# Last clipping on ScalarE, a warm-up matmul on a smaller cleared tile, and transfers of the tables in another order

## The reference, cut to what matters

```python
x = _L0_conv_ref(x, ...)   # relu(xWq), relu(xWk), xWv; softmax attention over 256 pixels; + x
x = _L1_conv_ref(x, ...)   # group norm, q, k, v, softmax attention over 256 pixels, Wo; x + h
x = _L2_conv_ref(x, ...)   # attention over 7 hexagonal neighbours, layer norm, feed-forward, layer norm
x = _L3_conv_ref(x, ...)   # 1x1 conv, 3x3 grouped conv, 1x1 conv, each with its affine; see below

# the end of _L3_conv_ref
out = lax.conv_general_dilated(h, w3, (1, 1), 'SAME', dimension_numbers=DN) + b3
return jax.nn.relu(out + x)
```

## Time and profile before

| what | value |
|---|---|
| median of 3 runs | 110.3 us (110.25 to 111.28) |
| the profiled execution, device time | 110.36 us |
| its span, first to last instruction | 108.3 us |
| TensorE matmul busy | 98.4 us |
| VectorE busy | 70.6 us |
| ScalarE busy | 54.2 us |
| GpSimd busy | 31.8 us |
| DMA traffic | 2.88 MB |

### The profile page before, as it was taken

How to read it: one execution, slowest core, us unless ns; L and a number is a source line. 1 busy time by engine, 2 the same in 40 slices (tenths; PEclk the granted TensorE clock), 3 DMA queues, 4 the chain that set the end, 5 groups by cost and what they waited for, 6 DMA issues and landing times.

```text
span 108.3 us, 2233 instructions
## 1 busy us (share of the span) xinstructions
PE 98.4 (91%) x834; PEld 51.9 (48%) x834; DVE 70.6 (65%) x166; ACT 54.2 (50%) x143; POOL 31.8 (29%) x46
## 2 busy tenths in 40 slices
PE   4978899899978999999989999999999998999960
PEld 1435768475646565453822563555322222467420
DVE  2029989989799958999999785498222522200292
ACT  2317969957989799991700400242367454200220
POOL 8960000919547910000004634962000201100000
PEclk9999999999999999999999999999999999999999
DMA  2991000000000000000000000000000000000005
GB/s 82 286 395 60 0 0 0 6 3 3 0 0 0 6 0 0 0 6 0 0 0 0 0 0 6 0 0 0 0 0 0 3 0 9 0 0 6 0 0 194
DMA packets 1594, 2.88 MB, mean 27 GB/s; under 512 B 176, under 2 KB 1200, under 8 KB 1584
## 3 DMA queue, kind: packets, MB, share of 16 engines
q1 hardware_dynamic: 1152, 2.09, 5.4%
q10 hardware_dynamic: 432, 0.67, 2.0%
HBM read 2.23 MB, written 0.52 MB: 25 GB/s over the span
## 4 chain that ended last, share of the span: by engine, by line
PE 54%; DVE 25%; ACT 7%; POOL 5%; issue 5%; POOLq 0%; ACTq 0%; DVEq 0%
PE quad L1097 6%; PE quad L1192 5%; PE bank L1117 4%; PE quad L933 4%; PE quad L1156 4%; DVE probn L672 4%; DVE nmax L663 3%; PE bank L1171 3%; PE bank L944 3%; ACT prob L438 3%; PE duo L1143 3%; PE bank L964 3%; PE duo L1192 3%; DVE ffh L262 2%; DVE ffh L741 2%
## 5 line engine op out<-in xcount | busy, mean ns | idle before, releaser
L438 ACT ACTIVATE prob<-quad,nmax 128x256 f32<-128x256 f32 x32 | 15.0, 483 | 2.5 <-DVE nmax L663 2.3
L944 PE MATMUL bank<-pv,probn 128*128 128x128 f32 x64 | 10.3, 283 | 1.7 <-DVE probn L672 1.1
L663 DVE TENSOR_REDUCE nmax<-quad 128x2 f32<-128x512 f32 x16 | 10.6, 682 | 1.5 <-PE quad L933 1.5
L672 DVE TENSOR_SCALAR probn<-prob,rrec 128x256 f32<-128x256 f32 x32 | 11.1, 390 | 0.6
L445 ACT ACTIVATE probT<-bank 128x512 f32<-128x512 f32 x16 | 9.6, 603 | 3.4 <-PE bank L944 3.2
L944 PEld LDWEIGHTS bank<-pv,probn 128*128 128x128 f32 x64 | 6.9, 141 | 6.1 <-DVE probn L672 3.7
L1192 PE MATMUL quad<-pads,ctaps 32*32 32x512 f32 x144 | 9.2, 595 | 0.0
L1192 PE MATMUL bank<-pads,ctaps 32*32 32x512 f32 x72 | 9.2, 596 | 0.0
L516 ACT ACTIVATE sq<-bank,prep2t 128x512 f32<-128x512 f32 x4 | 2.7, 687 | 12.3 <-PE bank L1117 9.3
L933 PE MATMUL quad<-k,q 32*128 32x256 f32 (+1 forms) x64 | 8.1, 400 | 0.9 <-ACT q L431 0.7
L1192 PE MATMUL duo<-pads,ctaps 32*32 32x512 f32 x72 | 8.8, 593 | 0.0
(11 more groups left out here) (184 smaller groups left out, 206.3 us busy)
## 6 DMA issues: line engine op xcount, KB each, us to landing
p<-in_p SPq DMA_DIRECT2D x1, 1012.5 KB, 7.0
xT<-in_xT SPq DMA_DIRECT2D x4, 128.0 KB, 4.0
p<-in_p ACTq DMA_DIRECT2D x1, 448.0 KB, 5.1
out_dram<-xT SPq DMA_DIRECT2D x1, 256.0 KB, 2.1
out_dram<-xT SPq DMA_DIRECT2D x2, 128.0 KB, 1.7
pv<-in_pv ACTq DMA_DIRECT2D x1, 128.0 KB, 3.2
p<-in_p ACTq DMA_DIRECT2D x1, 74.5 KB, 3.0
```

The costliest lines, as they stand in the source:

```text
L438: s.activation(prob[:, n % 3, b, :], S_BANK[n % 4][:, b * TOK:(b + 1) * TOK], ACT.Exp, bias=nmax[:, n, b:b + 1], accum_out=rsum[:, n, b:b ...
L663: v.tensor_reduce(nmax[:, n, :], S_BANK[n % 4].rearrange("p (b m) -> p b m", b=BLK), AX.X, ALU.max, negate=True).then_inc(max_ready, 1)
L672: v.tensor_scalar(probn[:, n % 2, b, :], prob[:, n % 3, b, :], rrec[:, n, b:b + 1], None, ALU.mult).then_inc(norm_done, 1)
L944: ins = nc.tensor.transpose(T_BANK[:, mb * TOK + b * 128:mb * TOK + b * 128 + 128], probn[:, n % 2, b, mb * 128:mb * 128 + 128], ident)
```

## The change

Three edits stand together.

- The clipping of the last results moves from VectorE to ScalarE. VectorE keeps the addition and raises a new semaphore `x3_sb`; ScalarE waits for it, clips with a Relu, and raises `fin_sb`.
- The tile `zeros` is cleared in two instructions, first 128 columns and then the other 520. The warm-up matmul waits for the first alone and reads those 128 columns four times as its moving operand of 512 columns.
- The pack pv is issued by SyncE between the second and third piece of x, no longer by ScalarE. On ScalarE p1 is issued behind the load of the activation table, no longer ahead of it.

```diff
@@ block.sync @@
             for j in range(PAIRS):
                 sp.dma_start(xT[:, j, :], xd[:, j, :]).then_inc(x_in[j], 16)
+                if j == 1:
+                    sp.dma_start(packed["pv"][:, :], t["pv"]).then_inc(tables_in["pv"], 16)
             sp.dma_start(packed["p2"][:, :], t["p2"]).then_inc(tables_in["p2"], 16)
@@ block.scalar @@
-            for p in ("p0", "pv", "p1"):
-                act.dma_start(packed[p][:, :], t[p]).then_inc(tables_in[p], 16)
+            act.dma_start(packed["p0"][:, :], t["p0"]).then_inc(tables_in["p0"], 16)
             s.preload_act_table_set("natural_log_exp_and_others")
+            act.dma_start(packed["p1"][:, :], t["p1"]).then_inc(tables_in["p1"], 16)
...
+            def finish(n):
+                columns = RESULTS[n][1]
+                act.wait_ge(x3_sb, n + 1)
+                s.activation(fin[:, columns], x3[:, columns], ACT.Relu).then_inc(fin_sb, 1)
...
             conv2_out(1)
+            for n in range(len(RESULTS)):
+                finish(n)
@@ block.vector @@
-            v.memset(zeros[:, :], 0.0).then_inc(zeros_ready, 1)
+            v.memset(zeros[:, 0:128], 0.0).then_inc(warm_ready, 1)
+            v.memset(zeros[:, 128:], 0.0).then_inc(zeros_ready, 1)
...
-            def finish(n):
+            def add_residual(n):
                 b, columns = RESULTS[n]
                 dve.wait_ge(c3_ps, n + 1)
                 dve.wait_ge(x2_ready, 1 + (n > 0))
-                done(v.tensor_tensor(x3[:, columns], b, x2.rearrange("p g n -> p (g n)")[:, columns], ALU.add))
-                v.tensor_scalar(fin[:, columns], x3[:, columns], 0.0, None, ALU.max).then_inc(fin_sb, 1)
+                v.tensor_tensor(x3[:, columns], b, x2.rearrange("p g n -> p (g n)")[:, columns], ALU.add)\
+                    .then_inc(x3_sb, 1)
...
             for n in range(len(RESULTS)):
-                finish(n)
+                add_residual(n)
@@ block.tensor @@
-                    mm(b, zeros[:, 0:128], zeros[:, 0:512], start=True, stop=True)
+                    mm(b, zeros[:, 0:128], rep(zeros[:, 0:128], 4), start=True, stop=True)
-            pe.wait_ge(zeros_ready, 1)
+            pe.wait_ge(warm_ready, 1)
```

More of the change, by code:

```diff
@@ L194, in build @@
         zeros_ready = sem("zeros_ready")
+        warm_ready = sem("warm_ready")
         zeroed = sem("zeroed")
@@ L238, in build @@
         rows_sb, lnb_ready = sem("rows_sb"), sem("lnb_ready")
-        c3_ps, fin_sb = sem("c3_ps"), sem("fin_sb")
+        c3_ps, x3_sb, fin_sb = sem("c3_ps"), sem("x3_sb"), sem("fin_sb")
         def col(name, k=0):
```

## The result

| kernel | median of 12 runs | range |
|---|---|---|
| before | 111.09 us | 110.25 to 112.25 |
| changed | 112.07 us | 111.66 to 126.88 |

The ratio of the changed kernel to the one before is 1.0104, with a 95% interval of 1.0063 to 1.0145. The change makes the kernel slower by about 1.2 us, where no difference was forecast. The three runs of before that the prediction had seen (median 110.3) were on the low side of a wide spread, and that turns out to be half of the story.

A forecast was written before the change was run, and what follows sets the result against it. TensorE was busy for 91% of the span, so only the start, held by GpSimd's selection, and the last stores could gain: 110.36 - 0.03 + 0 + 0 = 110.33, forecast 110.3 us, range 109.6 to 111.3.

The forecast's parts named there:

- Part 1, the clipping: At the end: third store issued 0.37 earlier, but stores share DMA engines, so the end moves only -0.03 us.
- the sum: Whole kernel: 110.36 - 0.03 + 0 + 0 = 110.33 us; at the end, third store's landing grows from 1.7 to 2.0 or more.
- Rival A: At the end: the stores don't hold each other up, so all 0.37 us is gained, 109.99; chance 0.16.
- the 0.63 and 0.74 that I took: ScalarE's clips at the end: 0.63 us for the first, 0.74 for the other two together.
- Part 2, the warm-up: At the start: warm-up begins 0.3 to 0.45 us earlier, but the projection still waits for p0; gain 0.
- rival B: At the start: longer TensorE pause before the projection, clock rises later, scores slow, 1.26 us lost, 111.59; chance 0.12.
- The sign that I had named: At the start: first scores taking over 2 us at 6.9 would show the late clock.
- Part 3, the transfers: At the start: later-issued transfers all have 0.5 us or more to spare before use; effect 0.
- a bound of +0.2: At the start: p1 issued at 1.2 competes with x piece 1, pushing keys and queries by about 0.2 us.
- rival D: At the start: x piece 1 lands late, queries after 6.45, time 110.5 us; chance 0.08.
- Rival C: At the start: faster clock or earlier p0 frees the start, gaining 1.4 us, 108.9; chance 0.04.

The follow-up runs named there:

- e2: The kernel before with only the smaller first cleared tile and the earlier warm-up; ratio 1.0073.
- e4: The changed kernel with p1 issued only behind ScalarE's wait on p0; ratio 1.0039 to the kernel before.
- e6: The kernel before with its old warm-up start but 256 columns of warm-up instead of 512; ratio 1.0103.
- e11: The changed kernel with the transfers in the order of before, so only the clipping and warm-up edits; ratio 1.0057 to the kernel before.
- e1: The kernel before with only the clipping moved to ScalarE; ratio 0.9995.
- e3: The kernel before with only the new order of transfers; ratio 1.0023.
- e5: The kernel before with the smaller tile and earlier warm-up, plus one more 128-column matmul behind it (640 columns in all); ratio 0.9993.
- e7: The kernel before with the early 640-column warm-up and a 128-column filler matmul between projection and first scores; ratio 0.9983.
- e8: The kernel before with the early 640-column warm-up, clipping on ScalarE and ScalarE's wait for consts moved later; ratio 0.9993.
- e9: The changed kernel with two more 128-column matmuls behind the warm-up; ratio 0.9965 to the kernel before.
- e10: The kernel before with clipping on ScalarE, early 640-column warm-up, filler before the scores and later consts wait; ratio 0.9955, then 0.9938 in a second set.
- e12: The changed kernel with two more warm-up matmuls, a filler before the scores and the later consts wait; ratio 0.9975 to the kernel before.
- e13: The kernel before with its warm-up begun later and cut to 384 columns, leaving no hole before the projection; ratio 1.0001.

## Why the prediction was wrong

**Part 1, the clipping: right.** The additions follow one another, the last issue comes earlier, and the small stores' time to landing grows from 1.7 to 2.0, as the sum had it. Alone its ratio is 0.9995. Rival A, a gain of 0.37, falls with the 2.0 and with the end that stays at 4.56 to 4.58. The clips were a little cheaper than the 0.63 and 0.74 that I took: 1.24 for all three. Yet the last issue came 107.49 - 105.24 = 2.25 behind the first addition, where it had been 106.18 - 103.68 = 2.50: 0.25 earlier and not 0.37, because SyncE's three issues now stand back to back, 1.32 for the three. The sum had no term for that; it made no difference.

**Part 2, the warm-up: the step that failed.** The term "Gain 0, with the clock as a risk (rival B)" was wrong: rival B is what happened, and I had given it 0.12. The warm-up started even earlier than the estimate, at 1.04 instead of 1.1 to 1.3, and the hole became 0.60 with the old transfers (e2) and 0.97 with the new ones, where I had 0.45. The sign that I had named, scores of over 2 us, is there (2.20 at 7.49). Without a filler behind the projection, the versions with a hole of 0.60 or more in their profile, the changed kernel among them, have 1 execution of 47 in the early group (e2 0 of 11, e4 1 of 7, e6 0 of 4, e11 0 of 10, the changed kernel 0 of 15). The versions whose profiles have 0.31 or less, e1, e3, e5, e7, e8, e9, the first set of e10, e12 and e13, have 58 of 90. The exception is the second set of e10: a hole of 0.82 in its profile, but a filler behind the projection, scores of 1.27, and 7 of 8 early. The hole is read from one profile of each version, and it varies with the landing of p0. The price of a late clock is the distance of the two groups, 1.0 us, where rival B had 1.26. Why it is less was not followed up. But the price is paid as a difference of chances: if the late group of before is one of late clocks, before pays it in 52 of 114 executions, and the changed kernel pays it always. That makes about 0.55 us in the mean from the clock alone.

Two readings led there. I treated the single execution of the profile as the kernel's one behaviour, though one of the three times was 0.98 higher, and I used that only to say that "something of this size comes and goes". And I weighed that activity begins 0.4 earlier against a longer hole without a row that ranks them. The rows of before could not rank them; e13 does, against e2. The Trainium skill ("TensorE: Matmul & The Clock Gate", section "What's actually happening") says that activity releases the throttle. I had read it as speaking for an earlier release when activity begins earlier, and the traces do not bear that reading out: in e2 activity began at 1.03 and was interrupted, and the scores were still slow; in e13 it began at 2.17 without a break, and they were fast.

**Part 3, the transfers: wrong in a sub-step.** The term was "All have 0.5 us or more to spare, so I take 0". I had left open whether ScalarE's sequencer waits for the table load, with p1 issued near 2.5 or near 1.2, and had made the second case a bound of +0.2. It does not wait: p1 was issued at 1.18, 0.03 into the load, where before it went out at 1.64 behind pv. x piece 1 then lands 3.4 to 3.9 after its issue in the five profiles with p1 early, and 2.8 to 3.6 in the eleven with the old order; with p1 held back (e4) it is 2.8. The ranges overlap, so that p1's rows are what delays it is likely and not shown. What was wrong is the time to spare. For x piece 1 it rested on first weights loaded at 4.65, but those were later loads of the same piece: its first came at 4.16, as it landed. A landing 0.4 later made the projection 0.41 longer in e3 and moved the queries from 6.29 to 6.65 (the projection had ended 0.12 before GpSimd did, at 6.13). That is rival D, to which I had given a price of 0.2 and a chance of 0.08; its sign, queries after 6.45, is there too (6.84). It costs 0.35 to 0.5 inside the changed kernel. That p0 also lands later is not shown to come from p1: with the old order it took between 2.9 and 3.6 us, with the new one between 3.0 and 3.5.

**Rival C** fell as argued: GpSimd held the queries until 6.25 even with a projection that was partly fast (e5, queries at 6.28), and moving the wait freed them (e10).

**The sum.** A median says little here, because that of before lies at the edge between two groups. In means the counted spans are 108.8 before, 109.5 for e11, 109.55 for e2 and 110.0 for the changed kernel. So the warm-up costs 0.7 to 0.8, of which the chances of the clock explain about 0.55, the order 0.4 to 0.5 and the clipping 0, together 1.2. The forecast of 110.3 also took over the low median of three runs; twelve gave 111.09. That is an error of 0.8 in the base and not in the mechanism: on 111.09 the sum would give 111.06, and 112.07 was measured.

**Open.** Why about half of the executions of before are late with a hole of 0.12, and 4 of 11 still with both holes filled, was not settled: it differs between executions of one program, and no run tests it. Two things scatter that could bear on it. p0 lands between 2.9 and 3.6 us after its issue, and in e7 and in the second set of e10 a late span came with transfers that landed late and not with a late clock. What a hole before the projection does when the one behind it is filled is open too.

## What to carry to other kernels

In this kernel the warm-up of TensorE was worth most when it lasted up to the first real matmul. So look at when that one's data land, and let the warm-up end there; if it is started earlier, make it longer by as much. Before calling a transfer harmless, find the first instruction that reads it, in a window narrow enough to show it alone. And when single runs fall into groups, find what tells them apart before pricing an edit by the profile of one of them.

## What the runs showed that was not expected

- With a hole of 0.60 us in TensorE's work before the projection (e2), 0 of 11 executions were in the early group; with 0.31 (e5) it was 6 of 10.
- The profile prints a granted clock of 1.00 for a stretch that runs at half speed, as the earlier trace rows did. The doubled duration of the same matmuls (2.20 against 1.26 for the scores) is what shows it. The window that holds the slow scores of the changed kernel (the clock is the third number from the end):

```profile
7.40:9.70 2.30, 2.21 (x18) 1.59 (x20) 0.14 (x1) 0.00 (x0) 0.00 (x0) 1.00 0.36 151
```

- ScalarE's sequencer issues a transfer while the engine loads its activation table: issue at 1.18, load from 1.15 for 1.28 us.
